# Four unread bf16 products on TensorE ahead of B's broadcast in groups 0, 6 and 7 of every chunk

## The chip, the cores and the metric

One Trainium2 chip, one of its cores. The metric is the time of one execution on the device in microseconds (us).

## What is computed

Two residual layers over x of 16 samples x 64 x 64 x 96, each on a group norm of its input (32 groups of 3 channels).

```python
# layer 0: upsample by 2 in the Fourier domain, W1, a polynomial, W2, low pass, every second pixel
h = xu @ W1.T + b1
h = coef[:, 0] + coef[:, 1] * h + coef[:, 2] * (h * h)
h = h @ W2.T + b2
# layer 1: a selective scan over the 4096 tokens of each sample
dA = exp(delta[..., None] * A)
dBu = delta[..., None] * Bm[:, :, None, :] * xc[..., None]
h = dA_t * h + dBu_t                        # 192 channels x 16 states, one step per token
y = einsum('bdn,bn->bd', h, C_t)
y = (ys + xc * D) * silu(z);  out = y @ W_out.T
```

## The kernel before

**Passages, chunks, groups.** A sample's scan is cut into NC8 = 8 chunks of T = 512 tokens. A chunk has NU = 24 units, n = 0 to 23, each 128 partitions (32 channels x 4 states) by 512 tokens, in NG = 8 groups of three, g = 0 to 7. A passage is the work from one sample's first chunk to the next one's; there are 16. While sample s is scanned, the layer-0 work of the samples after it (steps ST, SA, SB, W_up, W_f, W_2, W_dn, D_lo, D_hi and small ones for the norms) is laid between the units at positions 0 to 191 of the passage, by lists written in `stage_rows` and `mamba_rows`. The 15th passage has part of that work, the 16th none. Chunks are called chunk 0 to chunk 7 of a passage below.

**One unit.** ScalarE makes av = exp(delta A) (L883). VectorE makes, once a group, b (L1022) from rep_u and from pb, and then one scan a unit (L1028). GpSimd multiplies by C (L1069). TensorE sums over the states into py, three products a group (`reduce`, L757), each into its own strip of 32 partitions, 0 to 95; partitions 96 to 127 of py are used by nobody. VectorE reads py twice a chunk (`gate`, L1036).

**B's broadcast.** pb holds the group's B, spread to 128 partitions by one bf16 product of TensorE (`spread_b`, L746: 96 rows, 128 columns, 512 moved). pb is one PSUM bank without a second: the product of group g+1 waits until VectorE has made b of group g (`dve_bu`), and VectorE's next b waits for it (`pe_b`). VectorE has the three scans of group g meanwhile. TensorE issues the product of group g+1 at unit n = 3g+1; that of the next chunk's group 0 so comes at n = 22. "pb(g)" is that product, "b(g)" VectorE's multiplication with it.

**What stands between.** TensorE works its list strictly in the written order. At a position come first the unit's own instructions (pb at n % 3 = 1, `reduce` at n % 3 = 2), then the steps of that position. Positions 8 and 9 of a chunk carry X and Z (L710, L716: six and two f32 products of 512 columns), position 6 OUT (L737, L738), position 17 both DT (L725), whose results ScalarE turns into dlt (L873) at its own position 23, which frees the banks of the ring cb (three banks, taken in turn) for TensorE's steps that follow. In chunk 4 the norms and the first steps of the next layer-0 sample fall together (rows 88 to 105 of `stage_rows`).

Of the kernel before, what the change touches and what calls it, by code (L numbers as in the profile page):

```python
# [12 lines left out]
NS, HH, WW, C = 16, 64, 64, 96  # L13
# [18 lines left out]


BATCH = 8
AT = {
    "pe": dict(pb=1, red=5),
    "act": dict(xn=8, mid=23, batch=BATCH + 6),
    "dve": dict(y0=15, y1=3),
# [37 lines left out]
def even(steps, lo, hi):  # L76
    free = [p for p in range(lo, hi + 1) if not BATCH <= p % NU < BATCH + 2]
    return [(free[i * len(free) // len(steps)], st) for i, st in enumerate(steps)]


def mamba_rows(k, z_only=False):
    at = k * NU + BATCH
    x = [] if z_only else [("X", k, 0), ("X", k, 1)]
    rows = [(at, st) for st in x + [("Z", k, 0)]] + [(at + 1, ("Z", k, 1))]
    return rows + ([] if z_only else [(at + 5, ("DBC", k)), (at + 9, ("DT", k, 0)), (at + 9, ("DT", k, 1))])
# [55 lines left out]
def build(nc, A):  # L141
    ctx = ExitStack()
    with ctx:  # L143
        def sb(name, shape, dt=F32):
            return ctx.enter_context(nc.sbuf_tensor(name, shape, dt))

        def ps(name, shape):
            return ctx.enter_context(nc.psum_tensor(name, shape, F32))
# [38 lines left out]
        selb = sb("selb", [C, NQ, 128], BF16)  # L187
# [58 lines left out]
        py = ps("py", [128, 512])  # L246
# [86 lines left out]
        def ringed(plan):  # L333
            return sum(st[0] not in UNRINGED for _, st in plan)
# [9 lines left out]
        class Steps:  # L344


            def __init__(self, plan, base, thirds, s, prev=None, whole_w=False):
                self.plan, self.base, self.thirds, self.s, self.prev = plan, base, thirds, s, prev
                self.whole_w = whole_w
                self.at = {st: i for i, st in enumerate(st for _, st in plan if st[0] not in UNRINGED)}  # L350

            def find(self, st, user):

                if st in self.at and (st not in HEAD or user in HEAD or self.whole_w):
                    return self.at[st]
                before = {p: i for i, p in enumerate(p for _, p in self.prev if p[0] not in UNRINGED)}
                return before[st] - len(before)
# [46 lines left out]
        def count(sm, v):  # L404

            return max(v, 0)
# [8 lines left out]
        def _(sp):  # L415
# [109 lines left out]
            def a_part(st, k, n):  # L525
                s2, k2 = ahead(st.s, k)
                G2 = s2 * NC8 + k2
                at = AT["sp"]
                if n == 0 and G2 == 0:
# [14 lines left out]
            def c_part(st, k, n):  # L544
                G = st.s * NC8 + k
                at = AT["sp"]
                if not ((G < -1 or G + 1 >= NS * NC8)):
# [53 lines left out]
        def _(pe):  # L601
# [125 lines left out]
            def out(st, k, bank):  # L727
# [10 lines left out]
                    mm = pe.matmul(o, x1o[:, tb], ident[0:C, 0:C], start=False, stop=True)  # L738
                return mm

            def spread_b(G, k, g):

                if g == 0:
                    pe.wait_ge(pool_bc, count(pool_bc, G * 2 + 2))
                pe.wait_ge(dve_bu, count(dve_bu, G * NG + g))
                pe.matmul(pb[:, :], selb[:, g % NQ, :], bc3[:, k % 4, :], start=True, stop=True).then_inc(pe_b, 1)  # L746

            def reduce(s, k, g):
                G = s * NC8 + k
                hf, q = g // NQ, g % NQ  # L750
                pe.wait_ge(pool_hc, count(pool_hc, G * NU + 3 * g + 3))
                if q == 0:
                    pe.wait_ge(dve_y, count(dve_y, G * 2 + hf))
                    pe.matmul(py[0:C, :], ddiag[:, hf, :], xcs[:, k % 4, hf, :], start=True, stop=False,  # L754
                              skip_group_check=True)
                for j in range(3):
                    mm = pe.matmul(py[32 * j:32 * j + 32, :], rsel[:, :], hc[:, (3 * g + j) % NHC, :],  # L757
                                   start=False, stop=(q == NQ - 1), skip_group_check=True)
                mm.then_inc(pe_red, 1)

            def unit(s, k, n):
                G = s * NC8 + k
                if G == 0 and n == 0:
                    spread_b(G, k, 0)
                if n % 3 == AT["pe"]["pb"]:
                    if n // 3 + 1 < NG:
                        spread_b(G, k, n // 3 + 1)
                    elif not (G + 1 == NS * NC8):
                        spread_b(G + 1, k + 1, 0)
                if n % 3 == AT["pe"]["red"] % 3 and n >= AT["pe"]["red"]:  # L770
                    reduce(s, k, (n - AT["pe"]["red"]) // 3)

            def c_part(st, k, n):
                G = st.s * NC8 + k
                late = n + NU - AT["pe"]["red"]
                if late < NU and late % 3 == 0 and not (G < 1):
                    reduce(st.s + (k - 1) // NC8, (k - 1) % NC8, late // 3)

            run(lambda row: row[0], unit, step, lambda st, k, n: None, c_part)

        @block.scalar
# [391 lines left out]
```

## Time and profile before

| | us |
|---|---|
| median of 3 runs | 7217.09 (7207.39 to 7218.95) |
| the profiled execution | 7219.16 |
| its span, first to last instruction | 7217.5 |

| engine | busy us | share of the span |
|---|---|---|
| TensorE (PE) | 6447.3 | 89% |
| VectorE (DVE) | 5943.6 | 82% |
| ScalarE (ACT) | 4794.1 | 66% |
| GpSimd (POOL) | 4577.4 | 63% |

The busy share of an engine is a mean over stretches with different limits. The order of a chunk repeats 128 times, so the timelines of one passage are read chunk by chunk: a row with a bracket tells how long the engine stood idle before it and who ended that. TensorE's mean granted clock is 0.912 of full; of its two levels, 2.4 and 1.2 GHz, the lower one counts as 0.5. The first 331 us, before the first b, are set-up and the layer-0 work of the first samples.

### The profile page before, as it was taken

To read this page: it belongs to the slowest core of one execution; us is meant where nothing else is said; L and a number is where in the kernel's file an instruction comes from. 1 tells how busy PE (TensorE), PEld (TensorE's weight loads), DVE (VectorE), ACT (ScalarE), POOL (GpSimd) and SP (SyncE) were. 2 spreads that over 40 slices of the span, in tenths; PEclk is the share of its full clock that TensorE was granted. 3 is DMA by queue.
4 is the path that set the end of the run, shared out by engine and by line. 5 is a ranking of instruction groups with operands and counts; after the bars stand their busy time and mean duration, and the time that the engine had idled before them with its cause. 6 is when DMAs were issued, how large, how long until landed. Compare 5 with 4: busy or idle time off the path is not lost. (4 is left out here: it accounts for less than half of the span.)

```text
span 7217.5 us, 97516 instructions
## 1 busy us (share of the span) xinstructions
PE 6447.3 (89%) x32099; PEld 3299.1 (46%) x32099; DVE 5943.6 (82%) x4956; ACT 4794.1 (66%) x7986; POOL 4577.4 (63%) x4516
## 2 busy tenths in 40 slices
PE   7898998999898998999999899998999989898765
PEld 5545444444444444444444444444444444444211
DVE  0188888888888888888888888888888888889898
ACT  4576767667676776766667666676766767667554
POOL 0166666666666766667666666666766666677676
PEclk8998989999898998999999898998989999899776
DMA  3465655655655555565655555666555655555552
GB/s 89 112 151 134 146 141 129 148 136 146 148 136 141 140 143 137 145 147 131 150 130 147 143 134 140 138 150 144 136 146 132 150 137 145 144 129 142 121 122 68
DMA packets 805815, 983.15 MB, mean 136 GB/s; under 512 B 391258, under 2 KB 417542, under 8 KB 805318
## 3 DMA queue, kind: packets, MB, share of 16 engines
q1 hardware_dynamic: 805318, 976.92, 56.4%
q8 instruction: 264, 4.33, 0.3%
q14 instruction: 233, 1.91, 0.1%
HBM read 717.71 MB, written 259.00 MB: 135 GB/s over the span
## 5 line engine op out<-in xcount | busy, mean ns | idle before, releaser
L1069 POOL TENSOR_TENSOR hc<-hs,cs 128x512 f32<-128x512 f32 x3072 | 3843.5, 1269 | 2272.8 <-DVE hs L1028 1880.1
L1028 DVE TENSOR_TENSOR_SCAN hs<-av,state,b 128x512 f32<-128x512 f32 x2688 | 3282.4, 1264 | 83.5 <-DVE b L1022 2.7
L1022 DVE TENSOR_TENSOR b<-rep_u,pb 128x1536 f32<-128x1536 f32 x1024 | 1802.8, 1761 | 785.3 <-PE pb L746 721.2
L883 ACT ACTIVATE av<-rep_d,nega 128x512 f32<-128x512 f32 x3072 | 2129.2, 713 | 139.4 <-DVE hs L1028 134.9
L757 PE MATMUL py<-hc,rsel 128*32 128x512 f32 x6144 | 1227.4, 678 | 27.3 <-POOL hc L1069 27.2
L676 PEld LDWEIGHTS cb<-w2c,g 128*98 128x98 f32 x9600 | 937.6, 178 | 330.2 <-issue 267.9
L671 PE MATMUL cb<-xu,w1a 96*128 96x392 f32 x2400 | 1039.9, 529 | 50.1 <-ACT dlt L873 31.0
L676 PE MATMUL cb<-w2c,g 128*98 128x96 f32 x9600 | 990.2, 264 | 83.2 <-issue 55.4
L833 ACT ACTIVATE g<-cb,b1a 128x392 f32<-128x392 f32 x1200 | 695.7, 580 | 205.3 <-PE cb L671 189.5
L746 PE MATMUL pb<-bc,selb 96*128 96x512 bf16 x1024 | 416.4, 407 | 370.0 <-DVE b L1022 368.6
L710 PE MATMUL cb<-xn,wtap 96*96 96x512 f32 x1536 | 701.0, 606 | 0.3 <-DVE spare L966 0.3
L671 PEld LDWEIGHTS cb<-xu,w1a 96*128 96x128 f32 x2400 | 409.4, 194 | 547.8 <-issue 350.6
L1028 DVE TENSOR_TENSOR_SCAN hs<-av,zero_state,b 128x512 f32<-128x512 f32 x384 | 468.1, 1264 | 12.2 <-ACT av L883 0.6
L710 PEld LDWEIGHTS cb<-xn,wtap 96*96 96x96 f32 x1536 | 243.5, 165 | 468.7 <-issue 467.3
L857 ACT ACTIVATE xcs<-cb,tapb 96x512 f32<-96x512 f32 x256 | 174.9, 683 | 409.9 <-PE cb L710 409.9
L757 PEld LDWEIGHTS py<-hc,rsel 128*32 128x32 f32 x6144 | 161.8, 113 | 620.0 <-issue 449.4
L665 PE MATMUL cb<-up_h,t1r 128*96 128x196 f32 x1600 | 362.6, 351 | 50.7 <-DVE b1a L1000 46.8
L826 ACT ACTIVATE vr<-cb 98x384 f32<-98x384 f32 x400 | 194.3, 486 | 305.4 <-PE cb L676 304.0
L746 PEld LDWEIGHTS pb<-bc,selb 96*128 96x128 bf16 x1024 | 107.1, 105 | 618.2 <-DVE b L1022 393.3
L754 PE MATMUL py<-xcs,ddiag 96*96 96x512 f32 x512 | 296.3, 663 | 95.2 <-DVE xcs L1036 71.9
L737 PE MATMUL cb<-wo,xcs 96*128 96x96 f32 x2048 | 346.5, 297 | 0.8 <-issue 0.8
L826 ACT ACTIVATE xu<-cb 96x392 f32<-96x392 f32 x400 | 194.1, 485 | 221.5 <-PE cb L665 219.5
(102 smaller groups left out, 6525.5 us busy)
## 6 DMA issues: line engine op xcount, KB each, us to landing
rep_d<-delta_scratch SPq DMA_DIRECT2D x512, 384.0 KB, 6.2
rep_u<-deltax_scratch SPq DMA_DIRECT2D x512, 384.0 KB, 6.1
cs<-c_scratch SPq DMA_DIRECT2D x512, 256.0 KB, 6.1
delta_scratch<-dlt SPq DMA_DIRECT2D x128, 384.0 KB, 3.1
deltax_scratch<-dlt SPq DMA_DIRECT2D x128, 384.0 KB, 8.1
t_scratch<-t1s SPq DMA_DIRECT2D x128, 300.0 KB
t1r<-t_scratch SPq DMA_DIRECT2D x160, 240.0 KB, 5.0
rr<-v_scratch SPq DMA_DIRECT2D x256, 150.0 KB
```

Source lines behind the costliest of these rows:

```text
L665: mm = pe.matmul(bank[0:C, e * 2 * GH:(e + 1) * 2 * GH], t1r[:, m % 2, i2 % 5, :], up_h[:, :], start=True, stop=True)
L671: mm = pe.matmul(bank[:, 0:BC], w1a[:, 128 * f:128 * f + 128], xu[:, b % 2, :], start=True, stop=True)
L676: mm = pe.matmul(bank[0:GH, C * j:C * j + C], g2[:, b % 2, f, GH * j:GH * j + GH], w2c[:, f, :], start=(f == 0), stop=(f == NF - 1))
L710: mm = pe.matmul(bank[0:C, :], wtap[:, tap, t, :], xn[:, k2 % 2, tap:tap + T], start=(tap == 0), stop=(tap == 2))
L746: pe.matmul(pb[:, :], selb[:, g % NQ, :], bc3[:, k % 4, :], start=True, stop=True).then_inc(pe_b, 1)
L757: mm = pe.matmul(py[32 * j:32 * j + 32, :], rsel[:, :], hc[:, (3 * g + j) % NHC, :], start=False, stop=(q == NQ - 1), skip_group_check=True)
L826: act.activation(out, src, ACT.Copy).then_inc(fr, 1)
L833: act.activation(g2[:, b % 2, f, :], bank[:, 0:BC], ACT.Square, bias=b1a[:, f:f + 1]).then_inc(fr, 1)
L883: act.activation(av[:, n % NAV, :], rep_d[:, k % 2, j, :], ACT.Exp, scale=nega[:, q, j:j + 1])\
L1022: dve.tensor_tensor(b3[:, :, :], rep_u[:, k % 2, 3 * hf:3 * hf + 3, :], pb[:, None, :].broadcast_to([128, 3, T]), ALU.mult).then_inc(dve_b ...
L1028: dve.tensor_tensor_scan(hs[:, n % NHS, :], av[:, n % NAV, :], b3[:, n % 3, :], start, ALU.mult, ALU.add)\
L1069: pool.tensor_tensor(hc[:, n % NHC, :], hs[:, n % NHS, :], cs[:, k % 2, g % NQ, :], ALU.mult)\
```

## The change

`warm(times)` issues so many bf16 products of 96 rows, 32 columns and 512 moved elements into py's strip 96 to 127. They read selb, a constant, and nobody reads what they write. They wait for nothing and signal nobody. They stand ahead of the wait and of the product of `spread_b`, four of them at n = 1, n = 19 and n = 22, none at the other five places: 12 a chunk, 1536 in all.

```diff
+WARM = (4, 0, 0, 0, 0, 0, 4, 4)
...
+            def warm(times):
+
+                for _ in range(times):
+                    pe.matmul(py[C:128, :], selb[:, 0, 0:32], selb[:, :, :].rearrange("p q m -> p (q m)"),
+                              start=True, stop=True, skip_group_check=True)
...
                 if n % 3 == AT["pe"]["pb"]:
+                    warm(WARM[n // 3])
                     if n // 3 + 1 < NG:
                         spread_b(G, k, n // 3 + 1)
                     elif not (G + 1 == NS * NC8):
```

## Rows read from the trace of the kernel before

**Rows 1.** The page: busy time, share of the span and instructions by engine.

```profile
PE 6447.3 (89%) x32099; PEld 3299.1 (46%) x32099; DVE 5943.6 (82%) x4956; ACT 4794.1 (66%) x7986; POOL 4577.4 (63%) x4516
```

**Rows 2.** Who waited for whom, passages 1 to 14 (331 to 6421 us).

```profile
DVE b L1022 <- PE pb L746: 678.5, 302, 8.2
```

**Rows 3.** The same view for passage 7 alone (2937.5 to 3371 us).

```profile
DVE b L1022 <- PE pb L746: 45.6, 21, 6.7
```

**Rows 4.** Windows: length, busy by engine, PEclk, DMA; passages 1-14, 15, 16.

```profile
331.00:6420.00 6089.00, 5579.81 (x28047) 2878.13 (x28045) 5199.04 (x4314) 4176.93 (x6989) 4003.88 (x3946) 0.93 0.59 141
6420.00:6824.00 404.00, 337.48 (x1550) 154.16 (x1550) 361.87 (x290) 261.61 (x420) 285.10 (x281) 0.85 0.55 131
6824.00:7217.00 393.00, 250.40 (x850) 76.28 (x850) 354.96 (x274) 198.26 (x289) 279.65 (x279) 0.73 0.43 100
```

**Rows 5.** Timeline, VectorE: start, length, in brackets idle before; chunk boundaries of passage 7.

```profile
2992.63 1.76 DVE L1022 TENSOR_TENSOR b<-rep_u,pb 128x1536 f32<-128x1536 f32 x1 [1.96 <-PE pb L746]
...
3045.85 1.76 DVE L1022 TENSOR_TENSOR b<-rep_u,pb 128x1536 f32<-128x1536 f32 x1 [0.87 <-PE pb L746]
...
3071.89 1.76 DVE L1022 TENSOR_TENSOR b<-rep_u,pb 128x1536 f32<-128x1536 f32 x1 [2.86 <-PE pb L746]
...
3096.75 1.76 DVE L1022 TENSOR_TENSOR b<-rep_u,pb 128x1536 f32<-128x1536 f32 x1 [0.73 <-PE pb L746]
...
3216.43 1.76 DVE L1022 TENSOR_TENSOR b<-rep_u,pb 128x1536 f32<-128x1536 f32 x1 [0.60 <-PE pb L746]
...
3264.51 1.76 DVE L1022 TENSOR_TENSOR b<-rep_u,pb 128x1536 f32<-128x1536 f32 x1 [1.50 <-PE pb L746]
...
3366.03 1.76 DVE L1022 TENSOR_TENSOR b<-rep_u,pb 128x1536 f32<-128x1536 f32 x1 [1.21 <-PE pb L746]
```

**Rows 6.** Timeline, TensorE, passage 7: its waits beside the places of the change.

```profile
2941.29 0.39 PE L746 MATMUL pb<-bc,selb 96*128 96x512 bf16 x1 [2.54 <-DVE b L1022]
...
3002.44 1.07 PE L754 MATMUL py<-xcs,ddiag 96*96 96x512 f32 x2 [0.41 <-DVE xcs L1036]
...
3039.05 0.93 PE L671 MATMUL cb<-xu,w1a 96*128 96x392 f32 x2 [1.03 <-ACT dlt L873]
...
3043.22 2.32 PE L676 MATMUL cb<-w2c,g 128*98 128x96 f32 x24 [0.16 <-ACT g L833]
...
3147.86 0.59 PE L746 MATMUL pb<-bc,selb 96*128 96x512 bf16 x1 [4.11 <-DVE b L1022]
...
3260.22 3.93 PE L676 MATMUL cb<-w2c,g 128*98 128x96 f32 x24 [1.04 <-issue]
...
3273.40 0.39 PE L746 MATMUL pb<-bc,selb 96*128 96x512 bf16 x1 [2.65 <-DVE b L1022]
```

**Rows 7.** Timeline, TensorE, around 3500 us at the full clock.

```profile
3499.84 1.06 PE L757 MATMUL py<-hc,rsel 128*32 128x512 f32 x6
3500.83 5.39 PE L710 MATMUL cb<-xn,wtap 96*96 96x512 f32 x12
3506.06 1.88 PE L716 MATMUL cb<-xn,winz 96*96 96x512 f32 x4
```

**Rows 8.** Timeline, TensorE, groups 2 to 4 of passage 7's chunk 4.

```profile
3162.70 0.61 PE L746 MATMUL pb<-bc,selb 96*128 96x512 bf16 x1 [2.85 <-DVE b L1022]
...
3173.45 0.90 PE L665 MATMUL cb<-up_h,t1r 128*96 128x196 f32 x4 [3.43 <-DVE b1a L1000]
...
3181.19 1.93 PE L757 MATMUL py<-hc,rsel 128*32 128x512 f32 x6
3183.05 6.50 PE L710 MATMUL cb<-xn,wtap 96*96 96x512 f32 x12
```

**Rows 9.** Windows from pb(7) to pb(0) of chunk 0's end, passages 7 and 9.

```profile
2984.78:2992.16 7.38, 5.90 (x41) 3.44 (x39) 5.39 (x4) 6.95 (x12) 4.90 (x6) 1.00 0.33 92
3853.71:3865.06 11.35, 10.32 (x40) 5.94 (x39) 5.39 (x4) 7.19 (x12) 7.52 (x9) 0.55 0.40 104
```

**Rows 10.** Timeline, VectorE: the b(0) that ends the second of them.

```profile
3865.54 1.76 DVE L1022 TENSOR_TENSOR b<-rep_u,pb 128x1536 f32<-128x1536 f32 x1 [5.93 <-PE pb L746]
```

## The prediction

> **What bounds the kernel now.** I read the busy table first: TensorE is at 89%, VectorE at 82% [rows 1]. Neither is full, so the bound changes within a chunk, and the next question is who waits for whom. Over the 14 full passages VectorE stands 678.5 us idle before 302 of its b for TensorE's pb [rows 2]; in passage 7 alone it is 45.6 us before 21 of 64 [rows 3]. At those 21 places TensorE is the late one and its list is the critical path; at the others VectorE's b and scans are, and TensorE waits.
>
> So I followed passage 7's timelines chunk by chunk and marked, for each of the three places where the change adds work, which engine is late. Two kinds of rows answer that. A b with idle time released by pb says that TensorE was late: whatever is put ahead of that pb moves the b [rows 5]. A pb or another product with idle time released by VectorE or ScalarE says that TensorE was early: what is put ahead goes into the idle time, up to its length [rows 6]. One place is late in every chunk whatever happens: pb(4), behind X and Z, with 2.86 us in a typical chunk [rows 5]. So what TensorE loses between its last wait and pb(4) reaches VectorE there.
>
> **The change, part by part: the price of four products.** The trace of before has none of them, so I bound the price. The nearest row is pb itself, a bf16 product of the same 512 moved elements: 0.39 us when it stands alone at the full clock, 0.61 us at the half clock [rows 6, 8]. Going to half speed adds 0.22 us, which is the streaming part at full speed; the rest is latency that a follower hides. The f32 products agree: 12 records of X take 5.39 us and 4 of Z 1.88 us, so (5.39 - 1.88) / 8 = 0.44 us a record in a row [rows 7], two streams of 0.22. The four products have no dependence on one another, so I take 4 x 0.22 = **0.88 us** a place. The upper end is 4 x 0.39 = 1.56 us, if nothing overlaps. The lower end is 0: the three products of a `reduce` go to three strips and their six records take 1.06 us [rows 7], where three at 0.88 us each would take 2.64, so products in different strips do run side by side. I stay at 0.88, since the four share one strip and pb behind them fills all 128 columns; only what stands ahead of them could run beside them.
>
> The Trainium skill says in "TensorE: Matmul & The Clock Gate", Part 3, that tiles in different column groups run together; here the rows of `reduce` agree. By the rule taken widely the price would go toward 0 and the sum below with it, which is a rival below.
>
> **Where it lies on the path.** Boundaries are named by the chunk that begins.
>
> Into chunk 1. n = 19 stands ahead of pb(7), n = 22 ahead of pb(0). After pb(7) TensorE waits 1.03 us for dlt, whose DT products were issued before n = 19 (the same wait as the one shown at the next boundary [rows 6]). It absorbs the 0.88 us of n = 19 for TensorE. VectorE's b(7) may start later, but its next b(0) waits 1.96 us anyway [rows 5], so nothing remains. n = 22 has no wait behind it before pb(0): +0.88. n = 1 comes next: VectorE has slack at b(1), but TensorE's list is 0.88 later again and only one wait, 0.41 us for a gate [rows 6], lies before pb(4). Together 1.76 - 0.41 = 1.35 us.
>
> Into chunks 2 and 3. The same wait for dlt takes n = 19 [rows 6], b(0) waits 0.87 and 0.73 us for pb [rows 5], and no wait lies between pb(0) and pb(4): 1.76 us each.
>
> Into chunk 4. TensorE is early: it waits 4.11 us before pb(0), and 2.85 us before pb(2) after n = 1 [rows 6, 8]. All three groups of products vanish in these waits: 0. If that cover were gone it would be 2.64 us.
>
> Into chunk 5. b(0) waits 0.60 us for pb [rows 5]; n = 22 and n = 1 cost 1.76 us, less some 0.2 us of small waits: I take 1.55.
>
> Into chunks 6 and 0 (the ends of chunks 5 and 7). Here the wait for dlt stands ahead of the last W_2, so ahead of n = 19 (1.04 us before L676 [rows 6]), and does not cover it. b(7) waits 1.50 and 1.21 us for pb [rows 5]: +0.88 each. n = 22 and n = 1 then fall into the 2.65 and 2.54 us that TensorE waits before pb(1) [rows 6]: 0.
>
> Into chunk 7: no b at its beginning waits for pb: 0.
>
> Sum of a full passage: 1.35 + 1.76 + 1.76 + 1.55 + 0.88 + 0.88 = 8.2 us, times 14 = 115 us. In the 15th passage TensorE has 404 - 337 = 67 us idle, where an earlier one has (6089 - 5580) / 14 = 36 [rows 4]; I put it at 3 us. In the 16th it has 143 of 393 us idle [rows 4]: 0. Direct cost **118 us**. Nothing is moved on another queue: GpSimd and SyncE get no instruction, and ScalarE's and VectorE's steps are late only where TensorE is.
>
> **What the clock gives back.** In passages 1 to 14 the mean clock is 0.93 [rows 4], so TensorE spends 2 x 0.07 x 6089 = some 850 us at half speed. Part of it matters. Compare the same stretch, pb(7) to pb(0) at the end of chunk 0: in passage 7 at clock 1.00 it takes 7.38 us, in passage 9 at 0.55 it takes 11.35 [rows 9], and b(0) then waits 5.93 us instead of 1.96 [rows 10, 5]. The fall came after the wait for dlt. The products of n = 19 stand just before that wait and would raise TensorE's work there, so I expect many falls of this kind to be gone. How much such irregular falls cost in all: the 14 passages have 678.5 us of waits for pb, and 14 times passage 7, which has few such falls, would be 638 [rows 2, 3]. The difference is 40 us, and I take **30** of it back.
>
> The large cold stretch is chunk 4's, and it is not reached. Its cause is work that isn't there: waits of 4.11 and 2.85 us and one of 3.43 us before L665 [rows 6, 8]. Behind the last the clock falls again, and OUT, pb(3) and X run at half speed on the critical path, X in 6.50 us instead of 5.39 [rows 7, 8]. The products at n = 1 and n = 19 are groups away from it. Its length depends on where the fall lies against the burst, which a shift changes by chance: 0, give or take 20 us.
>
> The Trainium skill's rule in the same page, "Why this matters for your kernels", is to leave no long idle gap between bursts of matmuls; it speaks for the change. That waits precede the falls, the rows agree.
>
> **Sum.** 7219.2 + 118 - 30 = 7307 us for a profiled execution, which stood 2 us above the median: **7305 us**, 1.2% slower.
>
> **The rivals.** *The clock is held (faster, 18%).* If the fills keep the array at full speed through chunk 4 as well, the burst there gains X's 6.50 - 5.39 = 1.1 us, `reduce`'s 1.93 - 1.06 = 0.87, and and half of some 5.7 us that OUT and pb(3) take of the 7.7 us between L665 and that `reduce` [rows 8], 4.8 us in all, 67 us in 14 passages. Add all 40 us of the irregular part, and the W_2 of 3.93 us at the end of chunks 5 and 7, which takes 2.32 us at full speed [rows 6]: up to 1.6 us in some 22 places, 35 us. That is 142 us given back against 118: 7193 us; with products at half price 7135. It decides when the gain passes 8.4 us a passage. For it: half speed on the path is frequent. Against it: the fills end 0.9 us after they begin, and chunk 4's idle gaps are three to four times as long.
>
> *Side by side (no change, 12%).* The four products run partly beside the step ahead of them, or fall in waits too short for the rows; half price, 59 us, against 55 us of clock: some 7221 us. For it: `reduce`. Against it: most steps ahead of the places use all four strips.
>
> *Full latency (slower still, 10%).* Each product costs 0.39 us as alone, because a weight load stands before each: 118 x 1.56 / 0.88 = 209 us, less 30: 7398 us. For it: the lone pb; against it: the records of X and Z in a row.
>
> **How the numbers follow.** The likeliest case has 60%, its own range is 7260 to 7345 us (the clock's 0 to 60 us back, and chunk 4's chance). To hold 8 in 10 the range reaches down to the joint of the faster rival, 7195, and up to 7350. A measurement of this kernel tells 0.2%, some 14 us, from no change. Slower: 60 + 10 = 70%; same 12%; faster 18%.
>
> **What would show it.** In the changed kernel's timeline: four records in a row ahead of pb(1), pb(7) and pb(0) which together take 0.9 us; b(0) of chunks 1, 2, 3 and 5 later by 0.9 us against the b before; pb(0) of chunk 4 waiting 3.2 instead of 4.1 us; chunks 1 and 2 longer by 1.4 to 1.8 us; chunks 3 (its end) and 6 unchanged; chunk 4 still at a clock near 0.8. It is wrong if chunk 4's clock rises over 0.9, if the irregular falls cost more than 40 us, or if chunks 1 and 2 keep their length.

## The result

The changed kernel takes 7375.26 us in the median (7366.17 to 7405.69, 4 runs) against 7212.24 us (7202.28 to 7218.95, 4 runs): ratio **1.0235**, 95% interval 1.0202 to 1.0267. Slower was forecast, but by 88 us (118 - 30); it is 163 us, and 7375 lies outside the range that was given, 7195 to 7350. The executions of the kernel before, over all sessions, lie between 7172 and 7233 us. One execution of a kernel below, in_waits, took 14468 us; no view here explains it, and it is left out of that kernel's median and ratio.

A *fall* below is a drop of TensorE's granted clock from 2.4 to 1.2 GHz; work is *cold* while it runs at the lower level. How long TensorE is cold in a stretch is worked out from the granted clock there: at 0.80 over 65.5 us it is 2 x 0.20 x 65.5 = 26 us.

In the changed kernel the new products have line L746, pb L754, `reduce` L765, X L712, OUT L739 and L740, W_2 L678, and b L1031. The page answers to [rows 1] with:

```profile
PE 6774.6 (92%) x33635; PEld 3382.8 (46%) x33635; DVE 5946.5 (81%) x4956; ACT 4809.0 (65%) x7986; POOL 4576.9 (62%) x4516
...
L746 PE MATMUL py<-selb 96*32 96x512 bf16 x1536 | 439.6, 413 | 0.0
```

TensorE is busy 327 us longer and the span is 147 us longer. The waits over the 14 full passages, 338 to 6574 us, and the window of the same stretch answer to [rows 2, 4]:

```profile
DVE b L1031 <- PE pb L754: 836.7, 351, 8.2
...
338.00:6574.00 6236.00, 5878.14 (x29386) 2950.53 (x29385) 5201.53 (x4313) 4190.43 (x6987) 4003.36 (x3945) 0.94 0.57 138
```

VectorE waits 158 us longer for pb (678.5 before), and the 14 passages are 147 us longer. That is as much as the whole loss: it went into b's wait for TensorE.

The timeline of VectorE at passage 7's chunk boundaries answers to [rows 5] (start, length, in brackets the idle time):

```profile
3068.80 1.76 DVE L1031 TENSOR_TENSOR b<-rep_u,pb 128x1536 f32<-128x1536 f32 x1 [1.96 <-PE pb L754]
...
3115.74 1.76 DVE L1031 TENSOR_TENSOR b<-rep_u,pb 128x1536 f32<-128x1536 f32 x1 [2.25 <-PE pb L754]
3123.54 1.76 DVE L1031 TENSOR_TENSOR b<-rep_u,pb 128x1536 f32<-128x1536 f32 x1 [1.74 <-PE pb L754]
...
3176.58 1.76 DVE L1031 TENSOR_TENSOR b<-rep_u,pb 128x1536 f32<-128x1536 f32 x1 [0.75 <-PE pb L754]
3183.36 1.76 DVE L1031 TENSOR_TENSOR b<-rep_u,pb 128x1536 f32<-128x1536 f32 x1 [1.30 <-PE pb L754]
...
3299.43 1.76 DVE L1031 TENSOR_TENSOR b<-rep_u,pb 128x1536 f32<-128x1536 f32 x1 [1.68 <-PE pb L754]
...
3349.18 1.76 DVE L1031 TENSOR_TENSOR b<-rep_u,pb 128x1536 f32<-128x1536 f32 x1 [2.51 <-PE pb L754]
...
3451.87 1.76 DVE L1031 TENSOR_TENSOR b<-rep_u,pb 128x1536 f32<-128x1536 f32 x1 [2.43 <-PE pb L754]
```

The waits into chunks 2 (0.87 to 1.74) and 5 (0.60 to 1.68) and those at the ends of chunks 5 (1.50 to 2.51) and 7 (1.21 to 2.43) are each 0.9 to 1.2 us longer. Those into chunks 1 and 3 are not longer, because b(7) before them was itself late by as much.

TensorE's timeline at one boundary gives the price:

```profile
3113.49 0.93 PE L673 MATMUL cb<-xu,w1a 96*128 96x392 f32 x2
3114.35 1.04 PE L746 MATMUL py<-selb 96*32 96x512 bf16 x4
3115.32 0.39 PE L754 MATMUL pb<-bc,selb 96*128 96x512 bf16 x1
3115.67 0.93 PE L673 MATMUL cb<-xu,w1a 96*128 96x392 f32 x2
```

Four products take 0.97 us from start to start. They also start 0.86 us after the product ahead of them, where pb alone started 0.76 us after it (3036.87 to 3037.63 us in the kernel before). The kernel before has in that place:

```profile
3036.87 0.93 PE L671 MATMUL cb<-xu,w1a 96*128 96x392 f32 x2
3037.63 0.38 PE L746 MATMUL pb<-bc,selb 96*128 96x512 bf16 x1
```

The wait of b(7) grew by 1.07 us in chunks 0 and 1 (in the second from 1.18 to 2.25 us). So a place costs **1.07 us**, not 0.88; L673 next waits for nothing any more, where it waited 1.03 us for dlt [rows 6].

### The profile page after: what moved, and what is told of

Same layout as the page of the kernel before. It is cut to its first block and busy times, and to the rows that moved or that the text cites. A ratio compares the mean times of both kernels' runs of the same rounds, so it can differ in the third digit from the quotient of the medians.

```text
span 7364.5 us, 100588 instructions
## 1 busy us (share of the span) xinstructions
PE 6774.6 (92%) x33635; PEld 3382.8 (46%) x33635; DVE 5946.5 (81%) x4956; ACT 4809.0 (65%) x7986; POOL 4576.9 (62%) x4516
## 5 line engine op out<-in xcount | busy, mean ns | idle before, releaser
L1031 DVE TENSOR_TENSOR b<-rep_u,pb 128x1536 f32<-128x1536 f32 x1024 | 1803.5, 1761 | 934.1 <-PE pb L754 873.5
L765 PE MATMUL py<-hc,rsel 128*32 128x512 f32 x6144 | 1194.0, 661 | 16.6 <-POOL hc L1078 15.6
L673 PE MATMUL cb<-xu,w1a 96*128 96x392 f32 x2400 | 1036.9, 527 | 26.9 <-ACT vr L835 9.1
L678 PEld LDWEIGHTS cb<-w2c,g 128*98 128x98 f32 x9600 | 902.7, 173 | 303.6 <-issue 232.1
L678 PE MATMUL cb<-w2c,g 128*98 128x96 f32 x9600 | 956.2, 258 | 69.7 <-issue 44.2
L712 PE MATMUL cb<-xn,wtap 96*96 96x512 f32 x1536 | 707.5, 611 | 0.1
L754 PE MATMUL pb<-bc,selb 96*128 96x512 bf16 x1024 | 414.7, 405 | 275.4 <-DVE b L1031 272.9
L673 PEld LDWEIGHTS cb<-xu,w1a 96*128 96x128 f32 x2400 | 408.0, 193 | 503.1 <-issue 334.5
L712 PEld LDWEIGHTS cb<-xn,wtap 96*96 96x96 f32 x1536 | 246.0, 167 | 474.6 <-issue 473.4
L746 PE MATMUL py<-selb 96*32 96x512 bf16 x1536 | 439.6, 413 | 0.0
L765 PEld LDWEIGHTS py<-hc,rsel 128*32 128x32 f32 x6144 | 159.9, 112 | 600.4 <-issue 455.2
L754 PEld LDWEIGHTS pb<-bc,selb 96*128 96x128 bf16 x1024 | 105.1, 103 | 591.6 <-DVE b L1031 299.2
```

The costliest lines, as they stand in the source:

```text
L673: mm = pe.matmul(bank[:, 0:BC], w1a[:, 128 * f:128 * f + 128], xu[:, b % 2, :], start=True, stop=True)
L678: mm = pe.matmul(bank[0:GH, C * j:C * j + C], g2[:, b % 2, f, GH * j:GH * j + GH], w2c[:, f, :], start=(f == 0), stop=(f == NF - 1))
L712: mm = pe.matmul(bank[0:C, :], wtap[:, tap, t, :], xn[:, k2 % 2, tap:tap + T], start=(tap == 0), stop=(tap == 2))
L746: pe.matmul(py[C:128, :], selb[:, 0, 0:32], selb[:, :, :].rearrange("p q m -> p (q m)"), start=True, stop=True, skip_group_check=True)
L1031: dve.tensor_tensor(b3[:, :, :], rep_u[:, k % 2, 3 * hf:3 * hf + 3, :], pb[:, None, :].broadcast_to([128, 3, T]), ALU.mult).then_inc(dve_b ...
```

## Where it went, by chunk

This table is worked out from the starts of b(0) in each kernel's timeline: the mean length of a chunk over the 14 full passages, in us. Each row is one execution, the profiled one, and not the median: before's took 7219 us where its later medians are 7196 to 7201, gap_chunk4's 7155 where its median is 7182, only_n1's 7307 where its median is 7269. A difference of 1 us in a row is 14 us of a kernel, and executions of one kernel differ by more than that.

| kernel | chunks 0 to 3 | 4 | 5 | 6 | 7 |
|---|---|---|---|---|---|
| before | 215.6 | 63.8 | 54.5 | 49.9 | 51.0 |
| changed | 219.1 | 65.4 | 56.1 | 52.6 | 52.2 |
| only_n19 | 213.4 | 63.2 | 55.4 | 49.7 | 49.7 |
| only_n22 | 222.1 | 64.9 | 54.1 | 50.2 | 50.2 |
| only_n1 | 220.4 | 62.7 | 55.1 | 50.5 | 50.5 |
| chunks_0_3 | 220.0 | 63.3 | 54.7 | 50.2 | 50.2 |
| one_row | 223.4 | 65.6 | 55.6 | 49.6 | 51.0 |
| skip_chunk6 | 219.1 | 64.8 | 56.3 | 49.4 | 52.7 |
| late_off | 219.1 | 62.9 | 55.6 | 49.9 | 50.1 |
| beside | 216.1 | 63.3 | 54.6 | 49.5 | 50.8 |
| gap_chunk4 | 216.0 | 59.6 | 54.0 | 49.9 | 50.3 |
| dlt_waits | 213.9 | 61.7 | 54.0 | 49.9 | 48.3 |
| in_waits | 213.8 | 59.5 | 53.8 | 49.5 | 49.4 |
| in_waits_wide | 213.8 | 61.6 | 54.1 | 49.7 | 50.4 |

Changed against before: 3.5 us a passage in chunks 0 to 3, 7.1 in chunks 4 to 7, times 14 = 49 and 99 us. The 15th passage is 7 us shorter and the start 6 us later, which makes the 147 us. The prediction had 38 us for the first part (68 of direct cost less the clock's 30) and 46 for the second. The second is where it failed, and there mostly in one chunk: chunks 4 and 5 have 44 us where the direct sum gives 34, chunk 7 has 17 and 12, and chunk 6 has 38 us where it gives 0.

## The experiments

The kernel before was run anew beside these, with medians of 7196 to 7201 us. Ratios are to it.

**only_n19, only_n22, only_n1.** One place alone.

```diff
-WARM = (4, 0, 0, 0, 0, 0, 4, 4)
+WARM = (0, 0, 0, 0, 0, 0, 4, 0)      # only_n19
+WARM = (0, 0, 0, 0, 0, 0, 0, 4)      # only_n22
+WARM = (4, 0, 0, 0, 0, 0, 0, 0)      # only_n1
```

> The four products at n = 19 alone. Place theory (a place costs 1.07 us, as b(7) of chunk 1 moved in the changed kernel's trace, where TensorE is late and nothing behind it waits, and else nothing): on the path only at the ends of chunks 5 and 7, 2 x 1.07 x 14 = 30 us, less what the clock gives back after the wait for dlt in chunks 0 to 2, up to 40 us: 7200 to 7235 us. Price theory (every group of products costs its 1.07 us somewhere): 128 x 1.07 = 137 us for this place alone, 7350 us.

> The four products at n = 22 alone. Place theory: on the path into chunks 1, 2, 3 and 5, 4 x 1.07 x 14 = 60 us, clock 0 to 30 us back: 7240 to 7275 us, and b(7) not moved. Price theory: 7350 us. If instead most of the loss is cold time in the changed kernel's chunks 4 and 6, this kernel is at 7260 us with chunk 6 as long as before (49.4 us in most passages).

> The four products at n = 1 alone. Place theory: before pb(4) of chunks 1, 2, 3 and 5, less small waits, some 3.9 x 14 = 54 us: 7265 us. Cold-stretch theory (the products ahead of pb(1) in chunk 6 put off the clock's fall until it covers OUT and X of that chunk): chunk 6 is 57 to 59 us in some passages also here, and the kernel is at 7280 to 7320 us; if chunk 6 keeps its 49.4 us everywhere, that theory falls.

Measured: only_n19 0.9978 (0.996 to 0.9995), 7170 us; only_n22 1.0144 (1.0122 to 1.0165), 7295 us; only_n1 1.0097 (1.008 to 1.0114), 7269 us. That every group costs wherever it stands falls with the first: with 512 products ahead of pb(7) the kernel is no slower, and 0.2% faster, just outside the noise. Its window over chunks 0 to 3 of passage 7:

```profile
2927.30:3140.70 213.40, 201.85 (x1048) 99.60 (x1048) 183.93 (x151) 157.69 (x267) 143.98 (x142) 0.99 0.62 149
```

It is faster than I expected: the products go into the wait for dlt and chunks 0 to 3 are 2.2 us a passage shorter than before. In the table chunk 5 alone is longer, by 0.8 us. only_n22 is dearer than expected, 98 us over before instead of 30 to 60; in the table the excess is in chunks 0 to 3, 6.5 us a passage where three places cost 3.2; TensorE is cold there for 25 us a passage, 18 before. only_n1 costs 72 us where 54 were expected, and its chunk 6 has no passage over 52.6 us, so the cold-stretch theory in that form falls. Its start is there, though: in five of 14 passages the clock first falls 11 us after b(0) of chunk 6, where in before it first falls 1.9 to 3.3 us after it in all 14, and these five take 52.2 to 52.6 us instead of 49.4 to 51.2. The sum of the three is 144 us, near the whole.

**chunks_0_3.** The change in chunks 0 to 3 alone (`if k < 4` ahead of `warm`).

> All twelve products, but in chunks 0 to 3 of a passage alone. If the loss is the direct cost at late places, this kernel has three of the four boundaries: (1.7 + 2.1 + 2.1) x 14 = 82 us, less the 40 us of the irregular falls, all in these chunks: 7255 us. If the loss comes from cold stretches in chunks 4, 6 and 7 that a mere shift of the work against the clock causes, it stays: 7300 us or more.

Measured 1.0095 (1.0077 to 1.0113), 7266 us, 70 us over before where the direct theory had 42. So some 93 of the 163 us come with the places in chunks 4 to 7, where I had put 46.

**one_row.** The same number of products and of moved elements, with one row of operands instead of 96. py's unused strip gets other values.

```diff
-pe.matmul(py[C:128, :], selb[:, 0, 0:32], selb[:, :, :].rearrange("p q m -> p (q m)"),
+pe.matmul(py[C:128, :], selb[0:1, 0, 0:32], selb[0:1, :, :].rearrange("p q m -> p (q m)"),
```

> The changed kernel, but each of the extra products reads one row (partition) instead of 96: the same 512 moved elements and so the same time, with almost no multiplications. If the clock is held by TensorE being occupied, this is the changed kernel again, no cold time in chunks 0 to 2, 7360 us. If it is held by the multiplications, the cold time of chunks 0 to 2 returns (9 us a passage as before) and the kernel is slower than the changed one, 7380 to 7440 us, with chunks 0 to 3 longer.

Measured 1.0234 (1.0205 to 1.0262), 7370 us: the time of the changed kernel, with another clock. The windows of chunks 0 to 3 of passage 7, the changed kernel first, then one_row:

```profile
3014.80:3233.90 219.10, 210.00 (x1081) 101.72 (x1081) 183.91 (x150) 159.50 (x268) 143.86 (x142) 0.99 0.60 145
```

```profile
2994.20:3216.10 221.90, 217.27 (x1081) 103.49 (x1081) 183.92 (x150) 159.69 (x268) 143.89 (x142) 0.95 0.60 143
```

And TensorE of one_row at the end of chunk 1, where the clock falls at 3095.7 us, on the last of the products:

```profile
3094.87 1.14 PE L746 MATMUL py<-selb 1*32 1x512 bf16 x4
3095.94 0.61 PE L754 MATMUL pb<-bc,selb 96*128 96x512 bf16 x1
3096.34 1.52 PE L673 MATMUL cb<-xu,w1a 96*128 96x392 f32 x2
3097.79 1.93 PE L765 MATMUL py<-hc,rsel 128*32 128x512 f32 x6
```

The products of one row occupy TensorE as long (1.03 us a place at the full clock, 1.04 with 96 rows) and don't keep the clock here; those of 96 rows did. TensorE is cold for 10 us a passage in chunks 0 to 2, as before (9), and never in the changed kernel. That part went as the second theory said, the total did not: the clock's return is worth 4.3 us a passage in chunks 0 to 3 (223.4 against 219.1), and the changed kernel loses 4.5 us again in chunks 4 to 7 (226.3 against 221.8). In sum the clock returned nothing. Of the 4.5 us, 3.0 are in chunk 6, which takes 49.4 to 49.8 us in 13 of 14 passages of one_row and 52.2 in one.

**skip_chunk6.** Without the products at n = 22 of chunk 5 and n = 1 of chunk 6.

> The changed kernel without the products at n = 22 of chunk 5 and n = 1 of chunk 6, both of which fall into TensorE's wait ahead of pb(1) and cost nothing on the path. Shifted-fall theory (in the wait the clock falls later by the length of the products, and then covers OUT and X of chunk 6, which took 57 to 59 us in four of 14 passages of the changed kernel): chunk 6 returns to 49.4 to 51 us in all passages, 38 us less, some 7330 us. Chance theory (the falls of chunk 6 depend on where the whole passage lies): four to seven long chunks 6 stay, 7360 us.

Measured 1.0194 (1.0161 to 1.0226), 7342 us: 33 us less than the changed kernel (four executions of each, 7312 to 7371 and 7366 to 7406 us), and chunk 6 is 49.4 to 49.8 us in all 14 passages. In the changed kernel seven of its 14 take 52.4 us or more. The windows of chunk 6 in passage 3, the changed kernel first, then skip_chunk6:

```profile
1562.50:1619.90 57.40, 50.48 (x225) 24.28 (x224) 45.51 (x37) 33.43 (x56) 34.82 (x36) 0.85 0.39 88
```

```profile
1556.80:1606.20 49.40, 44.85 (x223) 21.66 (x224) 45.44 (x36) 33.25 (x55) 34.78 (x36) 0.93 0.46 103
```

And TensorE of the changed kernel there, from pb(1) on:

```profile
1564.35 0.39 PE L754 MATMUL pb<-bc,selb 96*128 96x512 bf16 x1 [1.51 <-DVE b L1031]
...
1574.28 1.99 PE L762 MATMUL py<-xcs,ddiag 96*96 96x512 f32 x2 [0.98 <-DVE xcs L1045]
1576.20 1.93 PE L765 MATMUL py<-hc,rsel 128*32 128x512 f32 x6
1578.06 2.98 PE L673 MATMUL cb<-xu,w1a 96*128 96x392 f32 x4
1580.83 1.01 PE L739 MATMUL cb<-wo,xcs 96*128 96x96 f32 x4
1581.63 0.63 PE L740 MATMUL cb<-ident,x1o 96*128 96x96 f32 x2
...
1586.46 1.93 PE L765 MATMUL py<-hc,rsel 128*32 128x512 f32 x6
1588.33 6.61 PE L712 MATMUL cb<-xn,wtap 96*96 96x512 f32 x12
```

From the gate's wait at 1574 us on everything runs at half speed until 2.5 us into X (1590.8 us), and OUT, pb(3) and X are the critical path to b(3) and b(4). The products did what they are for, they held the clock in the wait ahead of pb(1), where half speed would have cost nothing; the fall then came at the next waits. In the seven long passages the clock first falls 11.1 to 11.5 us after b(0), in the seven others 2.5 to 2.7 us after it; in skip_chunk6 it is 0.9 to 2.7 us in all 14, and in one_row, whose products stand in the same places, never later than 2.0 us where it falls in the chunk. So seven late falls in 14 passages go with products of many rows at these places. They are not enough by themselves: late_off, which keeps both places, has three late falls (chunk 6 at 51.0 to 52.3 us), only_n1 five, only_n22 one. What else decides is in part the end of chunk 5: in the seven short passages of the changed kernel the clock had fallen there, 11 us before b(0), and in six of the seven long ones it had not.

**late_off.** Without the products at n = 19 of chunks 5 and 7.

> The changed kernel without its products at n = 19 of chunks 5 and 7. In its trace they stand behind a W_2 that runs cold after the wait for dlt and take 1.6 to 1.9 us there instead of 1.0. Cold-product theory (the products themselves are stretched by the fall that precedes them): 2 x 1.7 x 14 = 48 us less, 7315 us. Plain place theory at the full clock: 2 x 1.07 x 14 = 30 us less, 7335 us. If b(7) is late there for another reason: 7360 us or more.

Measured 1.0141 (1.0106 to 1.0177), 7285 us: 90 us less than the changed kernel, where the theories give 60 and 40. The rows of the changed kernel at the end of chunk 5, then those of late_off:

```profile
3343.86 3.00 PE L678 MATMUL cb<-w2c,g 128*98 128x96 f32 x24 [1.03 <-issue]
3346.65 0.37 PE L651 MATMUL cb<-mv,gavg 96*96 96x1 f32 x2
3346.95 1.87 PE L746 MATMUL py<-selb 96*32 96x512 bf16 x4
3348.75 0.39 PE L754 MATMUL pb<-bc,selb 96*128 96x512 bf16 x1
```

```profile
3290.42 2.29 PE L678 MATMUL cb<-w2c,g 128*98 128x96 f32 x24 [1.04 <-issue]
3292.55 0.25 PE L651 MATMUL cb<-mv,gavg 96*96 96x1 f32 x2
3292.66 0.38 PE L754 MATMUL pb<-bc,selb 96*128 96x512 bf16 x1
```

Cold products are real: 1.87 us there, 1.58 at the end of chunk 7, and more than 1.4 us at each of the two places in seven of 14 passages; in the other seven they take 1.04. By the table chunks 5 and 7 are 0.5 and 2.1 us shorter, 37 us in 14 passages, between the two theories (28 places at 1.07 us, 30 us, and the 9 us that the cold ones took more make 39). The rest is 2.5 us in chunk 4 and 2.7 in chunk 6, neither of which this kernel changes: 73 us between the two profiled executions, 53 between the medians. That they moved because the passage arrives there at another time is argued, not shown; see below.

**beside.** The four products not ahead of pb but behind the three of `reduce`, for groups 5, 6 and 7.

```diff
                 mm.then_inc(pe_red, 1)
+                if g >= 5:
+                    warm(4)
...
-                    warm(WARM[n // 3])
```

> The twelve products of a chunk, not ahead of pb but right behind the three products of `reduce` of groups 5, 6 and 7, which fill strips 0 to 31, 32 to 63 and 64 to 95 only. Side-by-side theory (the four run in the fourth strip beside the `reduce`, as four records lie inside the reduce's 1.06 us in the changed kernel at 3223.6 us): price near 0.1 us a place, and the falls after the wait for dlt still avoided: 7150 to 7200 us, no slower than before. Serial theory (strips do not help, since TensorE takes products in order): as dear as in the changed kernel, 1 us a place and 7330 to 7380 us.

Measured 0.9998 (0.9983 to 1.0013): 1536 products for nothing. TensorE in chunk 2:

```profile
3043.13 0.63 PE L765 MATMUL py<-hc,rsel 128*32 128x512 f32 x3
3043.15 0.61 PE L746 MATMUL py<-selb 96*32 96x512 bf16 x2
3043.59 0.60 PE L765 MATMUL py<-hc,rsel 128*32 128x512 f32 x2
3043.59 0.38 PE L746 MATMUL py<-selb 96*32 96x512 bf16 x1
3043.60 0.59 PE L765 MATMUL py<-hc,rsel 128*32 128x512 f32 x1
3043.81 0.38 PE L746 MATMUL py<-selb 96*32 96x512 bf16 x1
```

All ten records lie within 1.06 us, the length of `reduce` alone: a product in the fourth strip is free right behind others in the first three. It was not free where the change has it. The Trainium skill says in "TensorE: Matmul & The Clock Gate", Part 3, that products in different column groups of the array run at the same time; these rows agree. The clock did not gain, though: TensorE is cold for 64 us a passage, 63 before. I read this from where the products stand, beside work and not in the wait; no run separates it.

**gap_chunk4.** None of the change's products; twelve behind the `reduce` at n = 5 of chunk 4, in the wait of 3.43 us [rows 8].

> No products at n = 1, 19, 22; twelve behind the `reduce` at n = 5 of chunk 4 alone, in the 3.43 us that TensorE waits there ahead of L667 for b1a. They take 2.9 us and cost nothing on the path. Reach theory: the fall of the clock that covers OUT, pb(3) and X of chunk 4 is avoided, chunk 4 goes from 63.8 to some 59 us: 4.8 x 14 = 67 us faster, 7130 us. If the fall has another cause (it comes from the earlier waits, or needs more than being occupied), chunk 4 keeps its 63.8 us: 7197 us.

Measured 0.9974 (0.9958 to 0.999), 7182 us. Chunk 4 takes 58.6 us in 11 of 14 passages and 63.4 in three, 59.6 in the mean, as the reach theory says. These 59 us are won between two single executions, before's at 7219 us and this one's at 7155; the medians differ by 20 us only. The end of chunk 4's wait, passage 4:

```profile
1871.66 2.10 PE L746 MATMUL py<-selb 96*32 96x512 bf16 x9
1875.45 0.90 PE L667 MATMUL cb<-up_h,t1r 128*96 128x196 f32 x4 [1.68 <-DVE b1a L1010]
```

Behind it OUT's four pairs take 2.7 us, at the full clock, where they took 5.1 in chunk 4 of before's passage 7.

**dlt_waits, in_waits, in_waits_wide.** Products only inside waits: four behind pb(7), ahead of the step that waits for dlt, in chunks 0, 1, 2 and 4, and four ahead of the last W_2 in chunks 5 and 7. The prediction and the texts below call the latter a wait for dlt too. It is not: in the trace of before that W_2 starts at 3260.22 us, when ScalarE's g (L833) is done at 3260.12, and dlt begins only at 3261.43.

```diff
-WARM = (4, 0, 0, 0, 0, 0, 4, 4)
+WARM = {(0, 19): 4, (1, 19): 4, (2, 19): 4, (4, 19): 4, (5, 18): 4, (7, 18): 4}        # dlt_waits
+                                                       # in_waits: also (4, 5): 12
+               # in_waits_wide: also (0, 0): 8, (3, 20): 14, (4, 0): 4, (4, 3): 10
...
                 if n % 3 == AT["pe"]["red"] % 3 and n >= AT["pe"]["red"]:
                     reduce(s, k, (n - AT["pe"]["red"]) // 3)
+                warm(WARM.get((k, n), 0))
```

> Products only inside waits that TensorE has anyway: four behind pb(7) in chunks 0, 1, 2 and 4 and four ahead of the last W_2 in chunks 5 and 7 (both in the 1.03 us wait for dlt), twelve in the 3.43 us wait of chunk 4. Theory (a product in a wait costs nothing and keeps the clock up through it): 20 us from chunk 4 as measured alone, some 26 us as with n = 19 alone, and up to 1.5 us at each end of chunks 5 and 7: 7120 to 7150 us. Rival (falls avoided at one place come at another, the sum of cold time on the path stays): 7180 to 7200 us.

> The kernel before this one plus fills for the long waits ahead of chunk 4's pb(0), pb(1) and pb(2) (14, 4 and 10 products) and eight ahead of pb(1) of chunk 0. If the clock can be held through the whole of chunk 4, chunk 4 takes 58.6 us in every passage and its clock is near 1.0: 10 to 30 us less than the kernel before this one. If its fills make TensorE late, b(0) to b(2) of chunk 4 wait for pb and it is slower than that one.

> The kernel with products only in waits, without the twelve of chunk 4: 24 products a passage in the six waits for dlt that lie in chunks 0, 1, 2, 4, 5 and 7. If the two kinds of fills add up, this one gives what the full one gave beyond chunk 4 alone: 82 - 20 = some 60 us faster than before, 7135 us, with chunks 5 and 7 each 0.8 to 1.5 us shorter than before and chunk 4 at its old 63.8 us. If chunk 4's gain needs the others (or theirs needs it), this is nearer 7170 us, as n = 19 alone was.

Measured: dlt_waits 0.9911 (0.9889 to 0.9933), 7133 us; in_waits **0.9895** (0.9863 to 0.9927), 7113 us; in_waits_wide 0.9945 (0.9927 to 0.9964), 7157 us. dlt_waits and in_waits are faster than both the kernel before and the changed one; their intervals overlap, so what the twelve products of chunk 4 add to the others is not resolved. dlt_waits has the 7133 us that were expected, but not all in the expected places: chunk 7 is 2.7 us a passage shorter than before, chunk 5 0.5, and chunk 4, which has no new product ahead of its long stretch, 2.1. At the end of in_waits' chunk 5 the products fill the wait and W_2 starts as early as before, at full speed, where it took 3.93 us [rows 6]:

```profile
3215.22 1.04 PE L746 MATMUL py<-selb 96*32 96x512 bf16 x4
3216.34 2.29 PE L678 MATMUL cb<-w2c,g 128*98 128x96 f32 x24
3218.46 0.25 PE L651 MATMUL cb<-mv,gavg 96*96 96x1 f32 x2
3218.58 0.38 PE L754 MATMUL pb<-bc,selb 96*128 96x512 bf16 x1
```

The rival, that an avoided fall only comes back elsewhere, holds for in_waits_wide: 36 products more a passage in chunk 4's and chunk 0's waits cost 43 us, and its chunk 4 is at 61.6 us again. They did not make TensorE late, b(0) to b(2) of chunk 4 wait for no pb. They did hold the clock, TensorE is cold for 40 us a passage instead of in_waits' 44. But in ten of 14 passages a fall begins 19 to 22 us after b(0) of chunk 4, at OUT, pb(3) and X, where in_waits has one in two.

## Why the prediction was wrong

- **Who is late where**: right. b waits longer at the chunk boundaries that were named; pb(0) of chunk 4 still waits 4.11 us after its four products, which ran beside a `reduce` there. Chunks 0 to 3 cost 3.5 us a passage. Where most of the irregular falls are gone these four take 213.4 to 213.8 us (only_n19, in_waits), so the direct cost is some 5.5 us, 77 us in all, where the prediction's three boundaries came to 68. One wait was named wrongly, the one ahead of the last W_2 in chunks 5 and 7, which is for g and not for dlt; the sum does not change with it.
- **The price**: 0.88 us was 1.07. The four take 0.97 us in a row, and 0.10 us goes in front of them. The upper end of 1.56 was far off. On the 118 us this makes some 25 us.
- **The wait for dlt absorbs n = 19**: right: only_n19 is no slower than before.
- **The clock's 30 us back**: the place was right, and by the table the size too. In chunks 0 to 3 the changed kernel has no falls but the last, after pb(7) of chunk 3. Before's four take 2.2 us a passage over the 213.4 of only_n19, 31 us. That the number fits so well is in part luck, since it rests on single executions.
- **The step that failed** is the one into chunk 6: *n = 22 and n = 1 then fall into the 2.65 and 2.54 us that TensorE waits before pb(1): 0*. They do fall into that wait, but a product in a wait was not free: it put the fall off, from the wait onto OUT, pb(3) and X, in seven of 14 passages. Chunk 6 took 2.7 us a passage more, 38 us of the 53 by which chunks 4 to 7 missed (99 where the direct sum was 46). Without these products (skip_chunk6) all 14 take 49.4 to 49.8 us again, and the kernel's median is 33 us less, 7342 us, inside the range. At the other boundary that the step speaks of, into chunk 0, the 0 held: chunk 0 takes 54.0 us in both kernels.
- **Products behind a fall** were priced at full speed. At the ends of chunks 5 and 7 they take 1.4 to 1.9 us in seven of 14 passages, 9 us in all.
- ***Chunk 4's stretch is not reached: 0, give or take 20 us***: held. Its clock is 0.80 in both kernels, and TensorE is cold there for 26 us where it was 25.5. Of the 1.6 us that it grew, 1.1 are b(0)'s longer wait at its end (0.60 to 1.68). None of the signs of being wrong that the prediction gave came true: they watched chunks 1, 2 and 4 and the irregular falls. Of what it expected to see, *chunk 6 unchanged* failed.
- **The rival of full latency** named nearly the right time (7398 us) for another reason, which is luck. At the full clock a place took 1.04 us from its start to its end, not four times the lone 0.39.
- **Still open**: how much of chunk 4's and 6's change is a mechanism of the change and how much the position of the passage against the clock's falls. late_off and the changed kernel have the same code up to the end of chunk 4, and differ there by 2.5 us a passage, 35 us: by passage it takes 61.3 to 61.9 us in nine of 14 in the one and 65.5 to 66.4 in twelve of 14 in the other. late_off's 53 us beyond chunks 5 and 7 may be no more than that. I did not shift the passage alone, but the traces have a case near to it: chunks 0 to 4 of the 16th passage have the same code in the changed kernel and in skip_chunk6, and take 47.8 to 47.9 us each in the one, 51.2 to 51.4 in the other, with the falls in other places. So the same code takes 3.4 us a chunk more or less with where the falls lie. Why the passage keeps one position or the other was not looked into.

## What to carry to other kernels

Filler products that keep TensorE's clock belong inside a wait that TensorE has anyway, behind the last instruction it can issue and ahead of the one that waits, and not ahead of a product that is already late: here six groups a passage of the first kind took 0.9911 of the time before, and the changed kernel, which has both kinds, 1.0235. Count them against the length of the wait, and check what half speed would have cost right there: a fall that covers only idle time is best left alone, because holding it off can move it onto the critical path. The time at half speed is not the measure either; where it lies is (in_waits_wide has less of it than in_waits and is slower). The Trainium skill advises to leave no long idle gap between bursts of products ("TensorE: Matmul & The Clock Gate", "Why this matters for your kernels"). Here the gain came from six waits of about 1 us a passage (dlt_waits, 63 us faster), and filling the longest ones as well, up to 4.11 us, cost 43 us again (in_waits_wide against in_waits).

## What was not expected of the hardware

- Products that read one row kept TensorE occupied as long as those of 96 rows (four in 1.03 us at the full clock, against 1.04) and did not keep the clock where those did: 0.95 against 0.99 over four chunks.
- Bf16 products in the fourth column strip run beside f32 products in the other three at no cost that shows for 1536 products: ratio 0.9998 (0.9983 to 1.0013).
- At half speed OUT's four pairs take 1.28 us each instead of 0.67. In the chunk 6 shown they are 5.1 us of products without a gap, and the clock did not come back during them; it did during X behind them, at 1590.8 us, when TensorE had worked without a gap since 1574.3.
- The same kernel's executions differ by up to 61 us (before: 7172 to 7233 us), more than the 35 us by which chunk 4 differs between two kernels with the same code in it.
